# A two-layer transformer kernel: GpSimd adds the softmax weights of two key quarters, eight target slots for the expert rows, and first-layer products behind the value blocks

## What is computed

```python
xn = _layernorm(x)
x = x + L0_attn(xn) + L0_ffn(xn)     # linear causal attention with small MLPs for q, k, v; fp4-quantised gated FFN, I = 352
xn = _layernorm(x)
x = x + L1_attn(xn) + L1_ffn(xn)

def L1_attn(x):                      # 16 query heads of 64, one shared key and value head
    q = (x @ Wq + bq).reshape(B, S, 16, 64); k = x @ Wk + bk; v = x @ Wv + bv
    w = softmax(einsum('bshd,btd->bhst', q, k) / 8)
    return einsum('bhst,btd->bshd', w, v).reshape(B, S, 1024) @ Wo + bo

def L1_ffn(x):                       # 8 experts, the two best of each token
    ...
    h = gelu(einsum('bsf,efh->bseh', x, W1) + b1)
    return einsum of (h @ W2 + b2) with the two gates
```

## Time and profile before

| | |
|---|---|
| time, median of 3 executions | 1470.13 us (1468.08 to 1475.42) |
| the profiled execution | 1460.9 us, its span 1459.0 us |
| TensorE busy | 1300.1 us, 89% |
| VectorE busy | 1013.9 us, 69% |
| ScalarE busy | 708.1 us, 49% |
| GpSimd busy | 252.5 us, 17% |
| mean granted TensorE clock | 0.953 |

### The profile page before, as it was taken

How to read it: one execution, slowest core, us unless ns; L and a number is a source line. 1 busy time by engine, 2 the same in 40 slices (tenths; PEclk the granted TensorE clock), 3 DMA queues, 4 the chain that set the end, 5 groups by cost and what they waited for, 6 DMA issues and landing times.

```text
span 1459.0 us, 22233 instructions
## 1 busy us (share of the span) xinstructions
PE 1300.1 (89%) x7377; PEld 767.7 (53%) x7377; DVE 1013.9 (69%) x2393; ACT 708.1 (49%) x1300; POOL 252.5 (17%) x306
## 2 busy tenths in 40 slices
PE   4569888999999999999999999999998778979877
PEld 2335445555555555555555555555454466656634
DVE  7777776578757875787677767776776456666655
ACT  3136454544454445444545454545454464757531
POOL 3132222201010111011001200110002035242510
PEclk9579999999999999999999999999999899999989
DMA  2042442002000200020002000200003255445242
GB/s 72 14 130 93 128 139 103 31 17 77 24 29 17 82 22 26 17 82 24 24 17 82 26 23 17 82 27 21 16 18 113 78 167 171 135 157 163 72 154 59
DMA packets 72372, 100.26 MB, mean 69 GB/s; under 512 B 29196, under 2 KB 49228, under 8 KB 68292
## 3 DMA queue, kind: packets, MB, share of 16 engines
q1 hardware_dynamic: 59876, 70.69, 15.6%
q0 software_dynamic: 10192, 27.44, 5.8%
q10 hardware_dynamic: 2192, 0.71, 0.2%
HBM read 59.86 MB, written 38.68 MB: 68 GB/s over the span
## 4 chain that ended last, share of the span: by engine, by line
PE 61%; DVE 15%; issue 12%; POOL 6%; DMA 2%; SPq 2%; ACT 1%; DVEq 0%; POOLq 0%; ACTq 0%
PE bank L1423 13%; PE bank L1395 7%; PE bank L1351 6%; PE bank L1396 6%; PE bank L1434 6%; POOL y_rows L701 5%; PE bank L1455 4%; DVE mneg L990 3%; PE bank L1275 3%; PE bank L1259 3%; PE bank L1260 2%; PE bank L1261 2%; PE bank L1310 2%; DVE q_lm L984 2%; PE bank L1292 1%
## 5 line engine op out<-in xcount | busy, mean ns | idle before, releaser
L821 ACT ACTIVATE wide<-bank 128x512 f32<-128x512 f32 x512 | 301.5, 604 | 502.8 <-PE bank L1396 492.5
L990 DVE TENSOR_REDUCE mneg<-bank 128x1 f32<-128x512 f32 x512 | 347.4, 686 | 203.6 <-PE bank L1351 197.7
L1395 PE MATMUL bank<-q_hh,k_hl 128*128 128x512 f32 x512 | 236.2, 461 | 19.8 <-DMA q_lm<-mrow 18.2
L1423 PE MATMUL bank<-wide,v_w 128*32 128x512 f32 x2048 | 248.7, 604 | 0.5 <-issue 0.5
L1351 PE MATMUL bank<-k_hl,q_hh 128*128 128x512 f32 x512 | 208.5, 409 | 36.0 <-DVE mneg L990 22.1
L1396 PE MATMUL bank<-q_lm,k_h 65*128 65x512 f32 x512 | 204.2, 399 | 0.0
L1395 PEld LDWEIGHTS bank<-q_hh,k_hl 128*128 128x128 f32 x512 | 97.7, 191 | 151.6 <-issue 109.4
L1351 PEld LDWEIGHTS bank<-k_hl,q_hh 128*128 128x128 f32 x512 | 98.7, 193 | 73.7 <-issue 52.8
L631 POOL TENSOR_TENSOR rs<-rs,power 128x4 f32<-128x4 f32 x24 | 24.6, 1026 | 626.2 <-DVE rs L892 626.2
L1434 PE MATMUL bank<-wide,ones 128*32 128x512 f32 x992 | 129.1, 592 | 0.0
L701 POOL DMA_INDIRECT y_rows<-y_m,to_u x92 | 92.4, 1004 | 177.0 <-DVE y_m L1117 155.0
(11 more groups left out here) (230 smaller groups left out, 2001.4 us busy)
## 6 DMA issues: line engine op xcount, KB each, us to landing
w_t<-w_rows SPq DMA_DIRECT2D x23, 1024.0 KB
x_rows<-part_h POOLq DMA_DIRECT2D x65, 258.0 KB, 5.7
inv<-inverse_scratch SPq DMA_DIRECT2D x124, 128.0 KB, 3.0
w_rows<-w_t SPq DMA_DIRECT2D x8, 1024.0 KB, 4.9
x_m<-x_rows SPq DMA_DIRECT2D x23, 258.0 KB
stage<-in_L_ffn_W SPq DMA_DIRECT2D x16, 256.0 KB, 4.8
yab<-y_rows SPq DMA_DIRECT2D x8, 512.0 KB, 7.3
xin<-in_L_attn_x SPq DMA_DIRECT2D x8, 256.0 KB, 4.0
```

Source lines behind the costliest of these rows:

```text
L821: act.activation(wide[:, st.g % WIDE, :], ps, ACT.Exp, scale=SCALE1).then_inc(wide_full, 1)
L990: dve.tensor_reduce(mneg[:, (gh // 2) % 2, col:col + 1], ps[:], X, ALU.max, negate=True)\
L1395: pe.matmul(ps, k_hl[:, n, t], q_hh[:, gh % HEADS, :], start=True, stop=False)
L1423: pe.matmul(ps_out[0][rows, :], v_w[:, n, c, TILE * d:TILE * d + TILE], weights, start=(c == 0), stop=(c == TT - 1))
```

## The change

1. **Sums of ones.** For k % 4 = 2 and 3, GpSimd adds the newest `wide` tile of a head and the one two steps before it (the two key quarters) into `halves`, in two instructions of 256 columns. `values` then leaves the ones out of half 0, and in half 1 multiplies the four `halves` tiles with ones, once per pair. It waits for `added` before that, and counts `summed` behind it. ScalarE's exponential additionally waits for `added` before it overwrites a `wide` tile.
2. **GpSimd's order** now follows the list of steps: adds, roots (`ROOT_AT`), scatters (`SCATTER_AT`), zeroes (`ZERO_AT`), splits and the transfers of y, each at its step.
3. **Eight target slots** (`TO = 8`) for `to_u`; the tile's turn moves from c = 1 to c = 0, `tile_turned` to c = 2.
4. **`store_m`** moves from SP's queue to ScalarE's, behind `copy_m`.
5. **Tables.** `L0_AT` puts the first layer's products at k % 4 = 1, where they come directly behind the value block; `L0_DVE`, the place of `xq` quantisation and of the attention norm in `l0` of VectorE, and the order of `q` and `mx` within a step follow. The read of the landed rows moves from step 41 to 43.
6. **Memory.** To make room for `halves`, `part_l` lies over the first layer's weights, `stage` over two of the four `w_t` slots (so the split of weights uses two), and `zeros`, `xq`, `xqt` over `part_h`.

```diff
-    WT, XT, YT, YM = 4, 2, 2, 3
+    WT, XT, YT, YM, TO = 4, 2, 2, 3, 8
...
-    LANDED_AT = 41
+    LANDED_AT = 43
+    ROOT_AT = [-12, 22, 43]
+    ZERO_AT = [8, 9, 12, 13, 16, 17, 20, 21]
+    SCATTER_AT = [0, 0, 1, 1, 4, 4, 5, 5]
...
-        if st.g is None or st.g % TT != 1:
+        if st.g is None:
             return []
-        here = st.g // TT
-        return [(use, tile_of[i]) for use, i in (("tx", here + 1), ("ty", here - 2)) if i in tile_of]
+        here, c = divmod(st.g, TT)
+        use, i = {0: ("tx", here + 1), 2: ("ty", here - 2)}.get(c, (None, None))
+        return [(use, tile_of[i])] if i in tile_of else []
...
-            def store_m(gp_):
-                read_out(sp, ("mt", gp_))
-                at_ = (2 * gp_) % HEADS
...
+            def add(st):
+                half, b = st.k % PAIR // TT, st.k % 2
+                pair = st.r * (H // 2) + st.k // PAIR
+                pool.wait_ge(summed, pair)
+                pool.wait_ge(wide_full, st.g + 1)
+                for q in range(2):
+                    cols = slice(S // 2 * q, S // 2 * q + S // 2)
+                    last = pool.tensor_tensor(halves[:, half, b, cols], wide[:, (st.g - 2) % WIDE, cols],
+                                              wide[:, st.g % WIDE, cols], ALU.add)
+                last.then_inc(added, 1)
...
+            for st in steps:
+                if adds(st):
+                    add(st)
+                if st.kind in ("pre", "o"):
+                    for n, k in ((st.r + 1, st.k), (st.r + 2, st.k - ATT)):
+                        if k in ROOT_AT and 0 < n < NB:
+                            root()
+                    if st.kind == "o":
+                        for j, k in enumerate(SCATTER_AT):
+                            if st.k == k:
+                                scatter(st.r, j // TT, j % TT)
...
                 act.activation(mrow[:, pair % 2, :], ps[0:2 * TT, 0:P], ACT.Identity).then_inc(free, 1)
+                read_out(act, ("mt", pair))
+                at_ = (2 * pair) % HEADS
+                act.dma_start(q_lm[DK:DK + 1, at_:at_ + 2, :].bitcast(F32), mrow[:, pair % 2, :].bitcast(F32))\
+                   .then_inc(m_loaded[pair % 2], 16)
...
+                        if st.g - WIDE in add_of:
+                            act.wait_ge(added, add_of[st.g - WIDE])
...
-                if t >= WT:
-                    landed(dve, t - WT)
+                if t >= TO:
+                    landed(dve, t - TO)
...
-                for c in range(2 * half, 2 * half + 2):
+                        last.then_inc(second_done, 1)
+                if half == 0:
+                    return
+                emptied_before(("ps", pair))
+                pe.wait_ge(added, add_of[st.g])
+                for part in range(2):
                     for b in range(2):
...
+                            elif d == part:
+                                last = pe.matmul(ps_out[1][rows, :], ones[:], halves[:, part, b, :], start=True, stop=True)
+                last.then_inc(summed, 1)
```

235 lines of the change are left out of this document (126 added, 109 removed).

## The result

The changed kernel takes 1534.84 us (median of 4 executions, 1527.32 to 1535.95) where the kernel before takes 1471.0 on the same chip: a ratio of 1.042 (95% interval 1.038 to 1.046). The forecast was 1377 us, 1342 to 1428. It was wrong by 158 us, in sign too.

The account below looks back on a forecast made before the run. TensorE was taken to bound the middle rows, with waits in the expert tiles and for the store. Terms 57.4 - 14 + 34 + 12 + 3 = 92 us off 1460.9 gave 1369, as a median 1377 us, range 1342 to 1428.

Parts of the forecast that it names:

- The step that failed: First layer's new places and VectorE's table: same amount of work moved, at most 40 us better or worse, taken as 0.
- VectorE off the path: Middle rows: GpSimd's adds lock VectorE out for up to 12.6 us a row, costing 2 a row, 14 over seven.
- The ones: Sums of ones on TensorE: one set less per ordinary pair, two less in the two last pairs, 57.4 us gained.
- The adds' own time: GpSimd's 256-column adds: 0.74 us each, done in time with 1.6 us of slack, costing the plain pair nothing.
- Rival C: The adds bind: at 1.75 us each the ones come 2.4 late, 154 us, median 1518; chance 0.05.
- Rival A: VectorE takes over in the rows: 130 of 137 us, rows stay near 143, median 1421; chance 0.20.
- B: Expert tiles stay slow near 9 us because another ring or the transfers bind: gain 10, median 1402; chance 0.15.
- Eight slots: Expert tiles: target waits go, a turn falls from 10.91 to 6.5 us, 34 us gained.
- The store: Store of the maxima on ScalarE's queue: 12 us gained of 18.2 us waited, between 0 and 18.
- Row 0: First row's extra 7 us: roots no longer queue behind splits; between +7 and -5, 3 us gained.
- forecast's own range: 1350 to 1398 us: 27 lower if three terms count in full, 21 higher with 5 us a row lost.
- D: Rival: the change does nothing measurable, all small losses together; chance 0.02.

Follow-up runs that it names:

- two_blocks_plain: Changed kernel without adds, first-layer products from step 12 on ahead of a value block, mostly two blocks before the next, VectorE's cuts between: 1402.52 us (0.959).
- behind_blocks: Kernel without adds and with the old tables, but four first-layer products and VectorE's first cuts on them one step later, behind the value blocks: 1501.16 us (1.027).
- rest_only: Changed kernel without GpSimd's adds and with the tables and order of before; slots, store and GpSimd's order stay new: 1390.96 us (0.946).
- adds_old_tables: Changed kernel with its adds, eight slots and store, but the tables and order of before: 1425.49 us (0.969).
- idle_adds: Kernel without adds and with the old tables, but GpSimd makes all adds and nobody reads them; TensorE sums all four quarters: 1455.01 us (0.990).
- rest_again: The kernel without adds and with the old tables, unchanged, timed once more beside another run: 1391.45 us (0.946).

## Why the prediction was wrong, point by point

**The step that failed** is "The first layer's new places and VectorE's table move work of the same amount; TensorE's air in a row is 143.6 - 137.9 = 5.7, so at most 5.7 x 7 = 40 better, and as much worse if a product waits for VectorE; I take 0." It measured +77 us without the adds and +110 with them. The work is of the same amount, but the price of a chain is set by what TensorE does while it runs: with the products ahead of a block and two blocks to the next one, 66 of the 77 us were gone (`two_blocks_plain`). What makes up the last 11, and why the tables cost 33 us more beside adds, stays open. The bound failed too. The air in a row limits what can be won; it says nothing about what can be lost. The rows that would have sized the loss stood in the trace of the kernel before. There the product (L1324) stands ahead of the block, VectorE's chain on it begins at 747.62, and the `q_lm` behind it ends at 751.77, before the block is through (751.95):

```profile
746.83 0.76 PE L1324 MATMUL bank<-wu,xqt 128*128 128x352 f32 x2
...
749.23 1.92 PE L1423 MATMUL bank<-wide,v_w 128*32 128x512 f32 x16
...
751.03 0.74 DVE L984 SCALAR_TENSOR_TENSOR q_lm<-bank,bq,q_hh 64x512 fp32r<-64x512 f32 x1
```

Behind the block it has short steps of 0.7 to 0.8 us to run beside, at four or five places a row. The order of the instructions showed the products behind the block, and I named them but put no time on it.

**VectorE off the path** was the second failing step: "between nothing and the 12.6 in full I take 2 us a row, nearer to nothing since VectorE is off the path, 14 us". The busy time was somewhat over-estimated (+7.7 to 9.3 us a row), the price far too low: 64 us while nobody used the sums. 39 us of air in a row is an average. VectorE was already on the path at two places, steps 33 and 59, where TensorE waited 1.34 us for a maximum and 1.37 us for `q_lm` before the change as well. At the second, 0.95 us more of that wait came with a step 2.4 us longer. The sentence at the end of the forecast ("I am wrong if VectorE's lock-outs hold up the small banks, so that TensorE waits for maxima and `q_lm`") names the mechanism; I had given it no chance and no price of its own.

**The clock** is in no term of my sum. In `behind_blocks` 10.0 us of waiting brought 6.8 us of slower work; in the changed kernel TensorE's busy time rose 1.9 us although 7 us of ones were gone.

**The ones**: 57.4 us forecast. In a plain block they gave what I read, 0.86 us (step 13 takes 4.43 us in `rest_only` and 3.56 in `adds_old_tables`). In all they gave 30. From `idle_adds` to `adds_old_tables` each of the eight blocks without ones is 0.8 to 0.9 us shorter, 6.9 us a row, but steps 39, 46 and 48 behind them take 1.5 us of it back, and row 0 gains nothing (147.9 to 149.3 us).

**The adds' own time** was right: 0.74 us at the median (713 to 1277 ns; the mean is 0.81), TensorE waited 1.2 us for them in the whole run. Rival C, the only one on the slower side, is refuted by that row, though the sign was its own. Rival A had the right engine and the wrong form: VectorE was to fill up to 130 us of a row and hold rows near 143; it has 114 of 160. B did not come about.

**Eight slots** 34 us: the three groups of tiles took 190.8 us before and 152.4 after, 38. **The store** 12 us: steps 0 to 15 of row 7 took 40.7 and then 27.6 in `rest_only`, steps 32 to 63 64.9 and then 58.1, together 20, just over the upper bound of 18. **Row 0** 3 us: 153.3 us before, 138.1 in `rest_only` and 142.6 in `rest_again`, so 11 to 15. These three were all taken too low; 49 forecast, some 70 measured. They are read from stages of the traces; none was taken out alone.

**The range.** The sentence on the forecast's own range says 27 us lower, but the terms that it names give 20 (4.6 for the 0.97, 9.3 for the 43.3, 6 for the 18). Its chances for the same time and for slower, 0.03 and 0.04, also do not match the 0.02 and 0.05 of rivals D and C. Neither decides anything here, as the measured time lies 107 us above the upper bound.
